# A kernel of two attention layers and four experts: batches pipelined in row tiles, with the causal mask of the maxima added by two 128-row matmuls per pair of heads

## The chip, the cores and the metric

The kernel runs on one core of one Trainium2 chip. The metric is the device time of one execution in microseconds (us), the median of the runs shown. Engines are named TensorE (PE in the profile, with PEld for its weight loads), VectorE (DVE), ScalarE (ACT), GpSimd (POOL) and SyncE (SP, here a queue of transfers).

## The reference

The input x has 8 batches of 512 tokens with 128 channels, in float32. Two layers with residuals follow each other. The first is a retention: layer norm, q, k and v of 16 heads of 8 channels, rotary angles, causal scores with a decay in place of a softmax, a norm per head, and an output projection. The second is a transformer block on the layer norm of the result: RMS norm, causal softmax attention with 16 heads of 8 channels whose q and k are normalised per head, then four experts with a router that keeps two of them. Channels 0 to 31 get neither attention nor expert output.

```python
qk = jnp.einsum('bhtd,bhsd->bhts', q, k) * (1.0 / np.sqrt(DH))
qk = qk * decay[None]
out = jnp.einsum('bhts,bhsd->bhtd', qk, v)
...
scores = jnp.einsum('bhqd,bhkd->bhqk', q, k) * HD ** (-0.5)
scores = jnp.where(causal[None, None], scores, -jnp.inf)
attn = jax.nn.softmax(scores, axis=-1)
...
o2 = _gelu(_gelu(_gelu(xf @ e2_l1.T) @ e2_l2.T) @ e2_l3.T) @ e2_l4.T
moe = wts[:, 0:1] * o0 + wts[:, 1:2] * o1 + wts[:, 2:3] * o2 + wts[:, 3:4] * o3
```

## The kernel before

**Tiles.** The 512 tokens of a batch are NT = 4 tiles of 128. The 16 heads are G = 4 groups of J = 4 heads. A head takes 32 rows of the contraction: q and k are split in a high and a low part, so that the one-pass float type (fp32r) is exact enough, and stand in `stack` as high, low, high, with the negated maximum of the row in a further row (SHIFT = 24). `stacked` transposes this layout with an identity matrix (L441): four matmuls for each group of q and of k, in both layers.

**Scores.** One matmul of 128 rows and 512 columns gives the scores of four heads for one pair of tiles: its moving operand (`qx` or `kx`) is spread in block form by transfers of SyncE, one per head (L1240, L1252), so that the rows of the other heads are zero. In the second layer every causal pair of tiles is computed twice, the queries in the rows for the maxima (L580) and the keys in the rows for the exponents (L593), 10 of each for each group. On the diagonal a second matmul adds the mask: idb times `negb` (L583) or times `negkb` (L596), in bf16, 128 rows and 512 columns. VectorE takes the maxima (L1058), ScalarE the exponents (L789). The maxima of a group are transposed (L602) and go into row SHIFT of `qx` by four small transfers (L1261). `weigh` multiplies the exponents with the values in column tiles of 32 (L560). The first layer does the same with the retained scores (L449), masked by VectorE (L957) and GpSimd (L1159), and `weigh_retained` (L460).

**Order.** All units of the second layer stand in one list, ORDER: the first NU + 14 maxima, then exponents and maxima in turn, then the last exponents. They rotate through four banks of PSUM (`pr`), so TensorE can be up to four units ahead of the engine that reads them. Two banks (`px`) serve what lies beside, one (`ps`) the single steps and one (`po`) the sums of values.

**Batches.** `run` has three stages. `beside_attention(b)` runs the attention of batch b with the down projections of b-1 and the `lead` of b+1 (layer norm, projections, rotation, stack and retained scores of tiles 0 and 1) beside it. `beside_front(b)` runs the rest of the first layer and the normalisations of b up to q and k of the second, with the expert matmuls of b-1 beside it (L629, L644; down projections L666). Batches 1 to 6 run in a hardware loop. Every engine works through its list in order and waits on semaphores, and inverse roots are eleven small VectorE steps (L876 to L881). All inputs of a batch are loaded by ScalarE's queue (L706).

## Time and profile before

| | us |
|---|---|
| median of 3 runs | 1051.71 |
| lowest and highest run | 1051.55, 1053.09 |
| the profiled execution | 1052.72 |
| its span | 1050.9 |
| busy: TensorE, VectorE, ScalarE, GpSimd | 866.0, 682.8, 507.0, 171.4 |
| mean granted TensorE clock, share of full speed | 0.899 |

A row of the profile names an engine, the line of the kernel, the operation, what is written and read, and how often. Times in a timeline are the start from the span's begin and the duration. Ends of matmuls are modelled and durations of neighbouring ones overlap, so what a matmul costs in a stream is read from the distance between starts. A float32 matmul stands there twice, once for each of its two passes, and each pass takes two cycles a column.

### The profile page before, as it was taken

What the parts mean: (1) busy time and instruction counts of PE and PEld (TensorE: products, weight loads), DVE (VectorE), ACT (ScalarE), POOL (GpSimd) and SP (SyncE); (2) the same over time, 40 slices, a digit from 0 to 9 for tenths busy, and PEclk for the clock granted to TensorE, in tenths of its full rate; (3) what the DMA queues carried; (4) which work ended last, traced back from release to release, by engine and by line L of the source; (5) the groups of instructions that cost most, each with busy time, mean ns of one, the idle gap of its engine ahead of it and who ended that gap; (6) DMA issues with size and microseconds to landing.
All of it is one profiled execution on the core that took longest, in us unless ns stands there. A gap on an engine that the chain in (4) does not pass through costs nothing.

```text
span 1050.9 us, 15987 instructions
## 1 busy us (share of the span) xinstructions
PE 866.0 (82%) x4513; PEld 500.2 (48%) x4560; DVE 682.8 (65%) x1825; ACT 507.0 (48%) x1080; POOL 171.4 (16%) x218
## 2 busy tenths in 40 slices
PE   2646897898878897898987897898977989879967
PEld 1524454464435554364543654455543645436434
DVE  6467936788368854789368873688457883578431
ACT  1313473456544474455644465454644556444634
POOL 5310202022010301013020210104020220202002
PEclk9575898899989998899988999799988989889979
DMA  4101210030100301021100301003100201003000
GB/s 142 40 11 24 47 33 20 1 71 13 41 11 0 81 5 46 0 50 31 40 11 0 81 1 40 11 10 71 29 22 0 59 22 40 1 0 81 2 0 11
DMA packets 27893, 31.57 MB, mean 30 GB/s; under 512 B 5184, under 2 KB 16064, under 8 KB 27840
## 3 DMA queue, kind: packets, MB, share of 16 engines
q1 hardware_dynamic: 23616, 28.92, 11.9%
q10 hardware_dynamic: 4224, 2.10, 0.7%
q8 instruction: 14, 0.23, 0.1%
q14 instruction: 39, 0.32, 0.1%
HBM read 5.58 MB, written 2.10 MB: 7 GB/s over the span
## 4 chain that ended last, share of the span: by engine, by line
PE 67%; DVE 20%; issue 6%; ACT 4%; DMA 1%; SPq 0%; DVEq 0%; POOL 0%; ACTq 0%; POOLq 0%
PE ring L593 9%; PE outs L560 8%; PE side L629 8%; DVE mxp L1058 6%; PE side L666 6%; PE ring L580 5%; PE ring L449 4%; PE ring L441 3%; PE side L644 3%; PE outs L460 3%; PE side L441 3%; PE single L435 2%; PE ring L596 2%; PE single L509 2%; PE ring L540 2%
## 5 line engine op out<-in xcount | busy, mean ns | idle before, releaser
L1058 DVE TENSOR_REDUCE mxp<-ring 128x4 f32<-128x512 f32 x320 | 204.8, 684 | 31.6 <-PE ring L580 25.6
L789 ACT ACTIVATE p<-ring 128x512 f32<-128x512 f32 x320 | 173.6, 603 | 67.5 <-PE ring L596 43.6
L593 PE MATMUL ring<-qx,ks 128*128 128x512 f32 x320 | 141.8, 497 | 20.7 <-DVE mxp L1058 19.2
L580 PE MATMUL ring<-kx,qs 128*128 128x512 f32 x320 | 147.3, 509 | 2.5 <-DVE mxp L1058 0.4
L1159 POOL TENSOR_SCALAR_AFFINE_SELECT p<-p 128x512 f32<-128x512 f32 x64 | 39.7, 635 | 311.9 <-ACT p L698 310.8
L593 PEld LDWEIGHTS ring<-qx,ks 128*128 128x128 f32 x320 | 62.4, 201 | 59.2 <-DVE mxp L1058 27.7
L560 PE MATMUL outs<-p,v 128*32 128x512 f32 (+3 forms) x1024 | 87.7, 442 | 0.7
L580 PEld LDWEIGHTS ring<-kx,qs 128*128 128x128 f32 x320 | 63.5, 202 | 37.2 <-DVE mxp L1058 23.8
L1053 DVE COPY oT<-outs 128x512 f32<-128x512 f32 x32 | 22.0, 689 | 89.7 <-PE outs L560 89.7
L435 PE MATMUL single<-sb_t_id,nat 128*128 128x128 f32 x128 | 27.2, 351 | 59.3 <-DVE nat L1086 29.6
L666 PE MATMUL side<-sb_w_dn,h 128*128 128x96 f32 x384 | 51.9, 276 | 6.0 <-ACT h L817 6.0
L1165 POOL TENSOR_TENSOR oT<-oT 128x192 f32<-128x192 f32 x32 | 18.9, 589 | 228.9 <-ACT oT L847 228.3
L435 PEld LDWEIGHTS single<-sb_t_id,nat 128*128 128x128 f32 x128 | 18.0, 176 | 79.7 <-issue 54.9
L666 PEld LDWEIGHTS side<-sb_w_dn,h 128*128 128x128 f32 x384 | 47.8, 192 | 13.8 <-ACT h L817 12.5
L449 PE MATMUL ring<-qx,ks 128*128 128x512 f32 x128 | 49.1, 519 | 3.1 <-DMA qx<-qs 3.1
L957 DVE TENSOR_TENSOR p<-ring,sb_t_tri 128x512 f32<-128x512 f32 x64 | 41.8, 686 | 13.8 <-PE ring L449 13.5
L817 ACT ACTIVATE hB<-side 128x512 f32<-128x512 f32 x32 | 19.1, 597 | 63.2 <-PE side L629 44.3
L698 ACT ACTIVATE p<-ring 128x512 f32<-128x512 f32 x64 | 36.1, 596 | 25.1 <-PE ring L449 24.9
L441 PE MATMUL ring<-idr,stack 128*128 128x128 f32 x256 | 37.4, 295 | 8.3 <-DVE stack L897 7.9
L596 PE MATMUL ring<-negkb,idb 128*128 128x512 bf16 x109 | 44.1, 405 | 0.0
L847 ACT ACTIVATE oT<-side,wts 128x96 f32<-128x96 f32 x128 | 32.3, 351 | 23.0 <-PE side L666 23.0
L560 PEld LDWEIGHTS outs<-p,v 128*32 128x32 f32 x1024 | 22.0, 108 | 43.9 <-issue 24.6
(169 smaller groups left out, 1602.2 us busy)
## 6 DMA issues: line engine op xcount, KB each, us to landing
qx<-qs SPq DMA_DIRECT2D x32, 256.0 KB, 4.6
...
qx<-h SPq DMA_DIRECT2D x128, 2.0 KB
...
```

Of the source, the lines that this page charges most:

```text
L435: last = nc.tensor.transpose(dst[:, t * 128:(t + 1) * 128], src(t), ident[:])
L441: last = nc.tensor.matmul(dst[:, t * 128:(t + 1) * 128], stack[:, s, t, J * g:J * g + J, :].rearrange("p j s -> p (j s)"), idr[:], start=T ...
L449: nc.tensor.matmul(dst[:, :], ks1[:, g, t * 128:(t + 1) * 128], qx[:, g, :, t * 128:(t + 1) * 128], start=True, stop=True)\
L560: last = nc.tensor.matmul(po[32 * j:32 * j + 32, kt * 128:T], v2[:, kt, h:h + SW], p2(kt)[:, j, :], start=kt == 0, stop=kt == NT - 1, skip ...
L580: last = nc.tensor.matmul(dst[:, :], qs[:, g, qt * 128:(qt + 1) * 128], kx[:, g % 2, :, kt * 128:(kt + 1) * 128], start=True, stop=kt < qt)
L593: last = nc.tensor.matmul(dst[:, :], ks[:, g, kt * 128:(kt + 1) * 128], qx[:, g, :, qt * 128:(qt + 1) * 128], start=True, stop=kt < qt)
L596: last = nc.tensor.matmul(dst[:, :], idb[:], negkb[:, :, :], start=False, stop=True)
L629: last = nc.tensor.matmul(dst[:, :], w[:, k * n + m * 128:k * n + (m + 1) * 128], src(k), start=k == 0, stop=k == blocks - 1)
L666: last = nc.tensor.matmul(dst[:, e * CM:(e + 1) * CM], h[:, k, t * 128:(t + 1) * 128], ww[w][:, k * CM:(k + 1) * CM], start=k == 0, stop=k ...
L789: A_(p2(kt)[:, :, (qt - kt) * 128:(qt - kt + 1) * 128], pr[(U_AB + at) % 4][:, :].rearrange("p (j n) -> p j n", j=J), ACT.Exp, scale=float ...
L957: V.tensor_tensor(p1[:, t % 2, g], src[:].rearrange("p (j n) -> p j n", j=J), tri[:].unsqueeze(1).broadcast_to([128, J, 128]), ALU.mult)\
L1058: V.tensor_reduce(mxp[:, qt, :, kt], ring(b, U_AB + at)[:].rearrange("p (j n) -> p j n", j=J), AX.X, ALU.max).then_inc(max_read, 1)
```

## The change

It replaces the three stages by one loop, written out in the program, of 12 iterations (`it` from -2 to 9). Iteration `it` works on five batches at once: `lead` of it+2 (layer norm, projections and rotation of the first layer), the retained scores and `before` of it+1 (rest of the first layer, normalisations), the maxima of `it`, exponents, output and router (`tail`) of it-1, and experts and down projections of it-2. An iteration has NF = 8 places, with experts, retained scores and `retain`, and then 32 steps. In step s TensorE computes one unit of exponents and one of maxima, then what the plan puts there. Exponents of groups 2 and 3 of batch it-1 come in steps 0 to 15, of groups 0 and 1 of batch `it` in steps 16 to 31.

A unit covers two heads and all tiles that a tile of 128 rows needs (128 to 512 columns). Each head has its own row tile of 32 rows (24 or 25 used) and its own bank. So q and k aren't spread in block form; the layout high, low, high comes from 12 transfers for q and 12 for k in each layer (`spread`), of 8 rows each, out of plain transposes whose high part ScalarE and whose low part VectorE or GpSimd writes. The mask of the maxima is two matmuls of 128 rows and 128 columns per unit (idb times `negb`). The exponents' mask is a GpSimd operation on the block of each unit. The maxima have two banks in all (`mb`), as have the exponents (`eb`), and each new unit waits until the last was read; three banks serve the rest. VectorE writes the negated maxima of a row at once. The norm per head takes its mean out with a matmul by `t_centre`. The outputs of two groups are summed in one bank. The diff, cut to its core (in `before` of SyncE, step 19 spreads for layer two; in `lead`, step 26 for layer one):

```diff
-ORDER = MAXIMA[:NU + AHEAD] + mixed(EXPS, MAXIMA[NU + AHEAD:]) + EXPS[(G - 1) * NU - AHEAD:]
...
+NH = J // 2
+CH = C
+GK = NT * NH
+LAG = 2 * GK
+FIRST, LAST = -2, B + 2
+
+WEIGH_AT = {5: (-1, 2, 0), 9: (-1, 2, 1), 13: (-1, 3, 0), 17: (-1, 3, 1), 21: (0, 0, 0), 25: (0, 0, 1), 29: (0, 1, 0)}
+MT_AT = {1: (-1, 3), 9: (0, 0), 17: (0, 1), 25: (0, 2)}
+NF = 8
...
+        mb = pb("maxima", [128, 2, 512])
+        eb = pb("scores", [128, 2, 512])
+        po = pb("outs", [128, 512])
+        px = [pb(f"side{i}", [128, 512]) for i in range(3)]
...
-        pr = [pb(f"ring{i}", [128, 512]) for i in range(4)]
-        ps = pb("single", [128, 512])
-        po = pb("outs", [128, 512])
-        px = [pb(f"side{i}", [128, 512]) for i in range(2)]
...
+            def maxima(b, k):
+                g, qt, hp = k // GK, k % GK // NH, k % NH
+                if k == 0:
+                    pe.wait_ge(spread2_q, count(spread2_q, b, 12 * 16))
+                    pe.wait_ge(spread2_k, count(spread2_k, b, 12 * 16))
+                if count(max_read, b, k) > 0:
+                    pe.wait_ge(max_read, count(max_read, b, k))
+                n = 128 * qt
+                for i in range(2):
+                    rows = slice(SW * (2 * hp + i), SW * (2 * hp + i) + SHIFT)
+                    nc.tensor.matmul(mb[:, i, 0:n + 128], qs[rows, b % 2, g, n:n + 128], ks[rows, b % 2, g, 0:n + 128],
+                                     start=True, stop=False, skip_group_check=True)
+                for i in range(2):
+                    last = nc.tensor.matmul(mb[:, i, n:n + 128], idb[:], negb[:], start=False, stop=True, skip_group_check=True)
+                last.then_inc(m_filled, 1)
...
+            def exponents(it, k):
+                b, g, kt, hp = scores_at(it, k)
+                if not on(b):
+                    return
+                i8 = GK * g + NH * kt + hp
+                if i8 % GK == 0:
+                    pe.wait_ge(shift_ready[g], count(shift_ready[g], b, J * 16))
+                if count(exp_done, b, i8) > 0:
+                    pe.wait_ge(exp_done, count(exp_done, b, i8))
+                n = T - 128 * kt
+                for i in range(2):
+                    rows = slice(SW * (2 * hp + i), SW * (2 * hp + i) + SHIFT + 1)
+                    last = nc.tensor.matmul(eb[:, i, 0:n], ks[rows, b % 2, g, 128 * kt:128 * kt + 128],
+                                            qs[rows, b % 2, g, 128 * kt:T], start=True, stop=True)
+                last.then_inc(e_filled, 1)
...
+            def retained_scores(b, t):
+                if t == 0:
+                    pe.wait_ge(spread1_q, count(spread1_q, b, 12 * 16))
+                    pe.wait_ge(spread1_k, count(spread1_k, b, 12 * 16))
+                at = slice(128 * t, 128 * t + 128)
+                for j in range(J):
+                    dst = side(f"SC{t}{j}", b)
+                    rows = slice(SW * j, SW * j + SHIFT)
+                    for g in range(G):
+                        last = nc.tensor.matmul(dst[:, 128 * g:128 * g + 128], ks1[rows, g, at], qs1[rows, g, at],
+                                                start=True, stop=True)
+                    last.then_inc(side_filled, 1)
...
+                for j in range(J):
+                    for g in range(G):
+                        w = SHIFT + SW * (J * g + j) - D * j
+                        last = nc.tensor.matmul(po[SW * g:SW * g + SW, at], v1x[:, t, w:w + SW],
+                                                p1[:, t % 2, j, 128 * g:128 * g + 128], start=t == 0 and j == 0, stop=j == J - 1,
+                                                skip_group_check=True)
...
+            for it in range(FIRST, LAST):
+                if it == FIRST + 1:
+                    pe.wait_ge(consts_made, 1)
+                    pe.wait_ge(loaded, 16 * (len(ww) + 7 - len(PROJECTION + ROTATION)))
+                for place in range(NF):
+                    if place in (0, 1, 3, 5) and on(it + 1):
+                        if place != 1:
+                            retained_scores(it + 1, (0, 1, 1, 2, 2, 3)[place])
+                    if place == 1:
+                        weigh(it - 1, 1, 1)
+                    if on(it - 2):
+                        experts(it - 2, place)
+                    if place == 1 and on(it + 1):
+                        retained_scores(it + 1, 1)
+                    if place in (2, 4, 6, 7) and on(it + 1):
+                        retain(it + 1, {2: 0, 4: 1, 6: 2, 7: 3}[place])
+                for s in range(G * GK):
+                    exponents(it, s)
+                    if on(it):
+                        maxima(it, s)
+                    if s in WEIGH_AT:
+                        off, g, half = WEIGH_AT[s]
+                        weigh(it + off, g, half)
+                    if s in (0, 2, 4) and on(it - 2):
+                        down(it - 2, s // 2)
+                    if on(it + 1) and s != 17:
+                        before(it + 1, s)
+                    if s == 6 and on(it - 2):
+                        down(it - 2, 3)
+                    if s in MT_AT and on(it + MT_AT[s][0]):
+                        maxima_transposed(it + MT_AT[s][0], MT_AT[s][1])
+                    if on(it + 1) and s == 17:
+                        before(it + 1, s)
+                    if on(it - 1):
+                        tail(it - 1, s)
...
+                g, qt, hp = k // GK, k % GK // NH, k % NH
+                dve.wait_ge(m_filled, count(m_filled, b, k + 1))
+                if k % GK == 0 and b:
+                    dve.wait_ge(mT_ready, count(mT_ready, b - 1, g + 1))
+                V.tensor_reduce(mneg[:, g, 2 * hp:2 * hp + 2, qt], mb[:, :, 0:128 * (qt + 1)], AX.X, ALU.max, negate=True)\
+                    .then_inc(max_read, 1)
...
+            def exponents(it, k):
+                b, g, kt, hp = scores_at(it, k)
+                if not on(b):
+                    return
+                i8 = GK * g + NH * kt + hp
+                pool.wait_ge(exp_done, count(exp_done, b, i8 + 1))
+                diag = p2[kt][:, 2 * hp:2 * hp + 2, 0:128]
+                Q.affine_select(out=diag, in_=diag, compare_op=ALU.is_ge, fill=0.0, base=0, pattern=[[0, 2], [1, 128]],
+                                channel_multiplier=-1).then_inc(exp_masked, 1)
...
+            def spread(dst, parts, order, signal):
 
-                    sp.wait_ge(ring_filled, count(ring_filled, b, U_AB + PLACE["max", g - 2, NU - 1] + 1))
+                    for r, part in enumerate(order):
+                        sp.dma_start(dst[SW * j + D * r:SW * j + D * r + D, :, :].bitcast(f32),
+                                     parts[SW * j:SW * j + SW, part, :]).then_inc(signal, 16)
...
+            def before(b, s):
+                if s == 19:
+                    if b >= 2:
+                        sp.wait_ge(e_filled, count(e_filled, b - 2, G * GK))
+                    sp.wait_ge(low2_ready, count(low2_ready, b, 1))
+                    spread(qs[:, b % 2], qhl, (0, 0, 1), spread2_q)
+                    sp.wait_ge(low2_ready, count(low2_ready, b, 2))
+                    spread(ks[:, b % 2], khl, (0, 1, 0), spread2_k)
+
+            def lead(b, s):
+                if s == 26:
+                    if b:
+                        sp.wait_ge(side_filled, UNIT["SC33", b - 1] + 1)
+                    sp.wait_ge(low1_q, count(low1_q, b, 1))
+                    spread(qs1, qhl, (0, 0, 1), spread1_q)
+                    sp.wait_ge(high1_ready, count(high1_ready, b, 2))
+                    sp.wait_ge(low1_k, count(low1_k, b, 1))
+                    spread(ks1, khl, (0, 1, 0), spread1_k)
```

## Rows read from the trace of the kernel before

**Rows 1.** The page: busy time of the engines; shares of the chain that ended last.
```profile
PE 866.0 (82%) x4513; PEld 500.2 (48%) x4560; DVE 682.8 (65%) x1825; ACT 507.0 (48%) x1080; POOL 171.4 (16%) x218
...
PE 67%; DVE 20%; issue 6%; ACT 4%; DMA 1%; SPq 0%; DVEq 0%; POOL 0%; ACTq 0%; POOLq 0%
```
**Rows 2.** Input loads inside the loop: min/median/max ns, first and last start.
```profile
L706 ACTq MOVE x_in<-x_dram x6: 29/29/29, 170.9 to 779.3; - x6
```
**Rows 3.** Stretches: us, then busy time of the engines, clock, DMA.
```profile
core 0: us, PE busy (x) PEld busy (x) DVE busy (x) ACT busy (x) POOL busy (x), PEclk, DMA share, GB/s
343.40:465.10 121.70, 105.35 (x564) 60.73 (x568) 83.44 (x227) 62.67 (x134) 19.57 (x26) 0.92 0.12 28
416.00:430.00 14.00, 14.00 (x60) 6.56 (x60) 8.13 (x23) 6.19 (x12) 2.72 (x5) 0.79 0.04 12
465.00:523.00 58.00, 53.54 (x333) 29.68 (x338) 38.09 (x66) 35.47 (x79) 12.72 (x16) 1.00 0.23 51
```
**Rows 4.** Timeline (start, us, engine): loads of one stacked transpose.
```profile
460.58 0.53 PEld L441 LDWEIGHTS ring<-idr,stack 128*128 128x128 f32 x4
```
**Rows 5.** Line 1058: min/median/max ns, first and last start; group of line 789.
```profile
L1058 DVE TENSOR_REDUCE mxp<-ring x320: 674/682/695, 102.0 to 985.5; 128x4 f32<-128x512 f32 x160
...
L789 ACT ACTIVATE p<-ring 128x512 f32<-128x512 f32 x320 | 173.6, 603 | 67.5 <-PE ring L596 43.6 <-PE ring L593 13.7 <-remote 5.8
```
**Rows 6.** Timeline: retained scores at two clocks; loads of two matmuls in a stream.
```profile
406.88 1.17 PE L449 MATMUL ring<-qx,ks 128*128 128x512 f32 x4
...
416.16 2.05 PE L449 MATMUL ring<-qx,ks 128*128 128x512 f32 x4
...
512.49 0.42 PEld L593 LDWEIGHTS ring<-qx,ks 128*128 128x128 f32 x2
```
**Rows 7.** Timeline: full array, column tiles of 32, full array again.
```profile
517.86 0.19 PEld L593 LDWEIGHTS ring<-qx,ks 128*128 128x128 f32 x1 [0.21 <-ACT p L789]
518.41 0.19 PEld L560 LDWEIGHTS outs<-p,v 128*32 128x32 f32 x8 [0.37 <-issue]
518.44 1.06 PE L560 MATMUL outs<-p,v 128*32 128x512 f32 x8
...
519.44 0.19 PEld L593 LDWEIGHTS ring<-qx,ks 128*128 128x128 f32 x1 [0.84 <-ACT p L789]
...
520.79 1.56 PE L560 MATMUL outs<-p,v 128*32 128x384 f32 x24
```
**Rows 8.** Timeline: one unit of exponents with its mask, alone.
```profile
484.21 0.50 PE L593 MATMUL ring<-qx,ks 128*128 128x512 f32 x1 [2.76 <-DVE mxp L1058]
...
484.55 0.39 PE L596 MATMUL ring<-negkb,idb 128*128 128x512 bf16 x1
```
**Rows 9.** Timeline: down projections, projections of two tiles, an output projection.
```profile
405.99 1.10 PE L509 MATMUL single<-sb_w_o,chT 128*128 128x96 f32 x8
...
466.53 1.03 PE L666 MATMUL side<-sb_w_dn,h 128*128 128x96 f32 x8
...
475.19 1.45 PE L472 MATMUL side<-sb_w_qkv,chT 128*128 128x384 f32 x4
```
**Rows 10.** Groups by line: steps of inverse roots, busy us, mean ns, idle before.
```profile
L879 DVE TENSOR_TENSOR rs_t<-rs_y 128x4 f32<-128x4 f32 x48 | 7.8, 162 | 1.6
L879 DVE TENSOR_TENSOR rs_t<-rs_y 128x128 f32<-128x128 f32 x24 | 7.0, 293 | 0.8
```
**Rows 11.** Timeline: loads of two successive expert matmul passes of 512 columns.
```profile
443.53 0.19 PEld L629 LDWEIGHTS side<-hA,sb_w_l 128*128 128x128 f32 x1 [0.24 <-issue]
...
443.96 0.19 PEld L629 LDWEIGHTS side<-hA,sb_w_l 128*128 128x128 f32 x1 [0.24 <-issue]
```
**Rows 12.** Line 1252: issues of 64 KB transfers, min/median/max ns, and their landing.
```profile
L1252 SPq DMA_DIRECT2D kx<-ks x96: 507/590/1634, 96.6 to 969.4; - x96
...
DMA to landing us min/median/max: 2.0/2.0/3.4
```
**Rows 13.** Timeline: a small VectorE step beside a clearing by GpSimd.
```profile
5.09 6.93 POOL L1226 MEMSET qx<- 128x8192 f32 x1
...
5.77 6.28 DVE L906 TENSOR_SCALAR rs_v<-mv_in 128x4 f32<-128x4 f32 x1
```

1730 lines of the change are left out of this document (769 added, 961 removed).

## The prediction

> **What bounds the kernel now.** I read the page first. TensorE is busy 82% of the span and holds 67% of the chain that ended last, VectorE 20% [rows 1]. The input loads give the period: the six loads inside the loop lie 170.9 to 779.3 us, so one batch takes (779.3 - 170.9)/5 = 121.7 us, and 8 x 121.7 = 974 leaves 77 us for the filling and emptying of the pipeline [rows 2]. The table of stretches shows where TensorE isn't pressed: in one period it is busy 105.4 of 121.7 us. Before attention, where normalisations and experts run (416 to 430 for one), its clock is 0.79; within attention (465 to 523) it is busy 53.5 of 58 us at clock 1.00 [rows 3]. So the kernel is TensorE-bound in attention and bound by chains across engines before it.
>
> **What is removed.** The stacked transposes (68 per batch at 0.53/4 = 0.13 us) cost 9 us of TensorE per batch [rows 4]. Also gone are their copies on VectorE and ScalarE, the second step of the maxima and six blocks of transposes. The maxima (40 units a batch at 684 ns = 27.4 us) and the exponents (40 x 603 ns = 24.1 us) become 32 larger units each, over the same 20480 elements per partition [rows 5]. From 684 ns for 512 elements I take 0.15 us fixed plus 1.04 ns an element, so 256, 512, 768 and 1024 elements cost 0.42, 0.69, 0.95 and 1.22 us, 26 us a batch. ScalarE likewise needs 23 us. So neither reader gains much.
>
> **What a step of the new kernel costs.** Attention is 32 steps per iteration. A step has one pair of row-tile matmuls for the exponents, one pair for the maxima, then the two 128-row masks. The maxima have one pair of PSUM banks, so each unit waits until VectorE has read the last; the exponents wait likewise for ScalarE. Before, four banks turned. No row of before shows a row tile, so I bound it. A load and a 128-column matmul take 0.13 us together [rows 4], and two full matmuls of 512 columns in a row 0.42, so 512 columns stream in 0.21 us [rows 6]. A pair of mean length 320 costs two loads, 0.26, and 0.13 of streaming if both run side by side: two pairs 0.78, less one hidden load 0.65. Column tiles do run side by side: eight matmuls of 512 columns take 1.06 us [rows 7]. The masks are 2 x 0.05 plus a load of 0.05.
> The masks need the whole array and the scores a quarter of its rows, so the array changes shape twice a step. The nearest rows are the changes to and from column tiles: the last load before the change ends at 518.05, the first column-tile load starts at 518.41, and the next full load at 519.44, when the eight matmuls have ended (518.44 + 1.06 = 519.50); it isn't hidden [rows 7]. I price going in at 0.14 and coming out at 0.24, of which 0.1 is a load already counted: 0.29 a step. Sum: 0.65 + 0.16 + 0.29 = 1.1 us. Ends: 0.8 without any cost of the change of shape, 1.4 if the pairs also run one after another (+0.27).
> A sentence of the Trainium skill speaks against this change: "Mode switching requires drain" (TensorEngine Tiling (Array Packing), Key Properties). By that rule the step is 1.1 us, without it 0.8; the trace's column tiles agree, with load to load 0.36 us going in.
> On VectorE's path a unit is: release, loads and maxima pair 0.5, masks with change and pipeline 0.38, then the reduction 0.82: 1.75 us on average. The row of before for the same path is a maxima or exponent matmul from 484.21 to the masks' end at 484.94, 0.73 us [rows 8]. Before, four banks hid this; now only other work can.
>
> **TensorE beside the steps.** Down projections: 64 matmuls at 0.125 (eight in 1.03) = 8.0 us [rows 9]. Weighing: 1.06 us for the first tile of a group and 1.56 for the other three [rows 7], 10.5 a batch, of which 7 of 8 halves lie in the steps: 10 with changes of shape. Projections 4 x 1.45 = 5.8, eleven blocks of transposes, taken like the stacked ones at 0.53: 5.8, wo2 1.1, wo1 and the new centring matmul likewise [rows 9], gate 1.2, states 0.8, four transposed maxima 1.4. Sum 36; with 32 x 1.1 = 35, TensorE has 71 us in the steps.
> VectorE beside the reductions has 34 us, mostly chains of small steps: eleven of 0.17 to 0.29 us plus 0.035 between them per inverse root, five of those [rows 10]. So 60 us, and ScalarE 44.
>
> **Why the steps take longer than 71.** Each engine works through its own list in order, and TensorE can be only one step ahead of VectorE. So I walk the steps and take the longer engine of each stretch. Steps 0 to 6: TensorE, 7 x 1.1 = 7.7 and beside them 12.9 (down projections 8.0, centring and wo1 2.1, half a weighing 1.9, a transpose and a maxima transpose 0.9), plus 1 waiting for ScalarE between ON and WO1: 21.5. Steps 7 to 16: VectorE, reductions 8.2 and 17.8 of normalisation (sum and moments 2.0, root 2.6, two scalings 2.2, moments 1.3, root 2.4, scaling 1.1, sums 1.7, root 3.3, product 1.2; passes over 512 elements at 0.69), plus two units that nothing covers, 0.94 each: 28. Steps 17 to 31: TensorE, 16.5 and beside them 16.4 (weighings 5.5, transposes 4.9, projections 2.9, wo2 1.1, gate 1.2, states 0.8), plus 4 where steps 18 and 25 belong to VectorE: 37. Together 86.5 us.
>
> **The places before the steps.** Experts: 38 matmul passes at 0.43 = 16.3 us [rows 11]. Retained scores: 64 loads and 128-column matmuls in row tiles, 0.13 each: 8.5 (before 16 at 0.19 = 3). Retained values 4 x 1.4 with changes of shape, the last weighing 1.3: 32, with buffer waits 33.
> But the first thing TensorE does there is to wait for the spread of q and k: 24 transfers, which SyncE issues in step 26, where before there were 4 or 8 at a time. One issue takes 590 ns, landing 2.0 us [rows 12]. 24 x 0.59 + 2.0 = 16.2 us after step 26's ScalarE and GpSimd work (at about 76.5): 92.7, while the steps end at 86.5. TensorE stands for 6 us, and everything behind the wait with it. In before, the four score matmuls that came after a stretch with TensorE pauses took 2.05 instead of 1.17 us [rows 6], its lower clock level: 2 us more. An iteration is 86.5 + 6 + 35 = 127.5 us against 121.7.
>
> **The ends.** There are 12 iterations, -2 to 9. The first maxima begin after two iterations that are chains, estimated by the same rows: the spread lands at 50, retained scores 16, normalisations and projections 38 at low clock, spread 2 and then spread 1 of the next batch (29 us of issues): 147 us, against 102.0 before [rows 5]. Iteration 0: 75. Iteration 1, no experts: 102. Iterations 2 to 5: 4 x 127.5 = 510. Iteration 6, no spread for a later batch: 120. Iteration 7, no normalisations beside: 22 + 64 = 86. Iterations 8 and 9, experts and down projections twice with little beside: 94. Sum 1134 us of span. The profiled run of before took 1052.72 with a span of 1050.9, the median is 1051.71: I add 1 and say 1135.
>
> **Rivals.**
> Faster (R1): the engines overlap more than my walk allows. What the normalisations cost in chains before (the stretch at clock 0.79 [rows 3]) really lies beside attention work now, and steps take TensorE's 71 us instead of 86.5, with a few for waits: 73. Seven iterations have full steps: 1135 - 7 x 13.5 = 1040; if the change of shape costs half too, 256 x 0.145 less: 1003. I say 1010. It decides in the steps: 1135 - 1051.7 = 83 us over 8 x 32 steps, so from 0.33 us a step less than I say, the new kernel is faster. For it: VectorE's total falls from 84 to 72 us a batch, and TensorE's is no higher. Against it: one buffer each, where four stood.
> Slower still (R2): the two matmuls of a pair don't run side by side, 256 x 0.27 = 69 more: 1200. Only column tiles speak against it.
> R3: the waits and chains are as I say but the transfers stall nothing, since the previous work hides them: 7 x 8 less, 1080. It needs issues of under 0.3 us; none of 96 was under 507 ns [rows 12].
> R4: the change of shape is free, the rest as I say: 256 x 0.29 less, 1060. I count its share with R3.
> That the change doesn't do what it says is excluded by the diff: two full-row mask matmuls per pair stand there.
> One more unknown has both signs: GpSimd masks every exponent block now, 32 a batch, and small VectorE steps were held up while GpSimd ran (one step took 6.28 us beside a clearing of 6.93) [rows 13]. I take 0, the ends are -1 and +6 us an iteration. And the loop is written out: issue holds 6% of the chain, 63 us [rows 1], which bounds from above what the jumps of the hardware loop can cost; I take 0 here too, and against the other end that the longer program is fetched late at places.
>
> **Chances.** Forecast (1085 to 1180) 0.52; R1 0.25; R2 0.09; R3 and R4 0.11; within 0.2% of before 0.03. A measurement of this kernel can tell about 0.2% from no change. Faster 0.25, same 0.03, slower 0.72. The range runs from 1005, which takes in most of R1, to 1195.
>
> **What would show it.** Right: a period of 127 us between output sums; TensorE idle of 4 to 8 us before the first retained scores, ended by the spread's transfers; reductions waiting for the mask matmuls; loads of the masks' weights starting only 0.1 us after the row tiles' end; first maxima near 147. Wrong: loads hidden under the other shape's matmuls; VectorE or ScalarE busy in nearly every step; matmuls of a pair that start one full length apart (R2); a period under 117 (R1).

## The result, and the profile after

The changed kernel takes 1330.68 us (median of four runs, 1328.57 to 1346.79) against 1051.68 us for the kernel before in the same job: a ratio of 1.268, 95% interval 1.258 to 1.278. It is slower, as forecast, but by 279 us where I had said 83, and 1330 lies far outside my range of 1005 to 1195. One run of one experiment below (the second of bank) fell in a slower state, at a lower granted clock, and is left out of its comparison. All of this section is read from one profiled execution of 1330.73 us with a span of 1328.6.

The page of the changed kernel, by the lines that answer to [rows 1]: busy time, the clock in 40 slices, the queue of the transfers (packets, MB, share of 16 engines), and the chain that ended last by engine and by line.

```profile
PE 927.6 (70%) x5904; PEld 562.4 (42%) x5904; DVE 581.6 (44%) x1433; ACT 444.0 (33%) x912; POOL 276.3 (21%) x483
...
q1 hardware_dynamic: 29152, 33.19, 15.9%
...
PE 47%; DVE 18%; SPq 13%; issue 9%; DMA 8%; ACT 4%; POOL 1%; POOLq 0%; ACTq 0%; DVEq 0%
SPq L1126 12%; PE side L443 12%; PE outs L384 5%; DVE mneg L810 5%; DMA ks<-h 4%; PE side L404 4%; PE scores L365 4%; PE side L479 4%; PE outs L422 3%; PE maxima L347 3%; PE side L334 3%; DMA qs<-h 3%; PE maxima L350 2%; PE side L434 2%; PE side L429 2%
```

No engine that held the chain has grown much: VectorE fell from 683 to 582 us busy, TensorE rose from 866 to 928. GpSimd rose from 171 to 276, with 1% of the chain. But in the chain stands what had 1% before: SyncE's issues of the spread (line 1126, 12%) and its landings (`ks<-h` and `qs<-h`, 7%). That is a fifth of the time, some 250 us of chain, on the way of transfers.

The output stores, the first and the fifth (start, us, engine and line), give the period: (1069.61 - 476.59)/4 = 148.3 us, where the forecast was 127.5 and before had 121.7 [rows 2].

```profile
476.59 0.39 SPq L1157 DMA_DIRECT2D out_dram<-yout  x1
...
1069.61 0.38 SPq L1157 DMA_DIRECT2D out_dram<-yout  x1
```

The first maxima start at 188.2 us. I had said 147; before it was 102.0 [rows 5].

```profile
L810 DVE TENSOR_REDUCE mneg<-maxima x256: 417/820/1229, 188.2 to 1232.0; 128x2 f32<-128x256 f32 x32, 128x2 f32<-128x512 f32 x32, 128x2 f32<-128x768 f32 x32, 128x2 f32<-128x1024 f32 x32
```

Stretches of one iteration, as [rows 3]: the places with experts and retained scores, the 32 steps, the wait behind them, and the last part of that wait one iteration earlier.

```profile
core 0: us, PE busy (x) PEld busy (x) DVE busy (x) ACT busy (x) POOL busy (x), PEclk, DMA share, GB/s
706.40:744.20 37.80, 35.66 (x254) 19.32 (x254) 10.00 (x26) 14.89 (x23) 5.08 (x8) 0.81 0.00 1
744.20:840.00 95.80, 75.09 (x480) 47.35 (x476) 60.62 (x150) 39.16 (x88) 27.35 (x48) 0.74 0.17 26
840.00:855.40 15.40, 1.95 (x12) 0.93 (x12) 2.45 (x2) 0.87 (x3) 0.81 (x2) 0.61 0.61 77
...
697.60:706.40 8.80, 0.00 (x0) 0.00 (x0) 0.00 (x0) 0.00 (x0) 0.00 (x0) 0.50 0.65 79
```

38 us of places, 96 of steps, 15 of nothing. In the last row no engine does anything: the transfers alone run, at 79 GB/s. These are the spread's and the 256 KB of the next input, which SyncE issues right behind it. The spread alone shows in the middle of the second layer's (812 to 826 us), at 68 GB/s:

```profile
812.00:826.00 14.00, 10.42 (x61) 7.07 (x61) 8.57 (x23) 3.57 (x12) 4.81 (x6) 0.63 0.53 68
```

The clock shown in the wait is 0.50, its lower level of 1.2 GHz; it was 0.92 over a period before.

The queue of SyncE over the second half of an iteration shows both spreads, 12 transfers of q and 12 of k each:

```profile
802.50 8.49 SPq L1126 DMA_DIRECT2D qs<-h  x12
811.04 8.43 SPq L1126 DMA_DIRECT2D ks<-h  x12
...
831.72 8.49 SPq L1126 DMA_DIRECT2D qs<-h  x12
840.32 8.43 SPq L1126 DMA_DIRECT2D ks<-h  x12
```

and these are the two that wait for them, ScalarE in step 25, then TensorE in front of the retained scores (the brackets: idle before it, and what ended it):

```profile
827.59 0.60 ACT L712 ACTIVATE qT<-side 128x512 f32<-128x512 f32 x1 [6.07 <-DMA ks<-h]
```

```profile
706.44 1.14 PE L404 MATMUL side<-qs,ks 24*128 24x128 f32 x12 [16.31 <-issue]
...
856.51 1.14 PE L404 MATMUL side<-qs,ks 24*128 24x128 f32 x12 [13.50 <-issue]
```

The last issue of the second layer's spread ends at 819.47, and ScalarE goes on at 827.59: a landing 8.1 us behind the last issue. For the first layer's it is 848.75 and 856.51, 7.8 us. The 64 KB transfers of before landed in 2.0 [rows 12]. ScalarE waits at all since both layers put their high and low halves into the same buffers (`qhl, khl = h0, h3`), so layer 1 may not write until layer 2's spread has left. The wait at the retained scores is put down to issue, but the queue shows what it is: in all eight batches it ends 7.8 to 8.9 us after the last issue.

Summed over the run, TensorE's waits are these (us, times, longest):

```profile
PE maxima L347 <- DVE mneg L810: 107.7, 84, 2.6
PE side L404 <- issue: 87.6, 6, 16.3
PE side L404 <- DMA ks<-h: 66.0, 2, 39.6
```

154 us stand in front of the retained scores. ScalarE has 47.4 us more in step 25.

### The profile page after: what moved, and what is told of

Its sections match the earlier page's. It is cut to its first block, busy times and chain, and to the rows that moved or that the text cites. A ratio compares the mean times of both kernels' runs of the same rounds, so it can differ in the third digit from the quotient of the medians.

```text
span 1328.6 us, 16021 instructions
## 1 busy us (share of the span) xinstructions
PE 927.6 (70%) x5904; PEld 562.4 (42%) x5904; DVE 581.6 (44%) x1433; ACT 444.0 (33%) x912; POOL 276.3 (21%) x483
## 2 busy tenths in 40 slices
DMA packets 29228, 34.19 MB, mean 26 GB/s; under 512 B 5344, under 2 KB 16352, under 8 KB 29152
## 3 DMA queue, kind: packets, MB, share of 16 engines
q1 hardware_dynamic: 29152, 33.19, 15.9%
## 4 chain that ended last, share of the span: by engine, by line
PE 47%; DVE 18%; SPq 13%; issue 9%; DMA 8%; ACT 4%; POOL 1%; POOLq 0%; ACTq 0%; DVEq 0%
SPq L1126 12%; PE side L443 12%; PE outs L384 5%; DVE mneg L810 5%; DMA ks<-h 4%; PE side L404 4%; PE scores L365 4%; PE side L479 4%; PE outs L422 3%; PE maxima L347 3%; PE side L334 3%; DMA qs<-h 3%; PE maxima L350 2%; PE side L434 2%; PE side L429 2%
## 5 line engine op out<-in xcount | busy, mean ns | idle before, releaser
L810 DVE TENSOR_REDUCE mneg<-maxima 128x2 f32<-128x256 f32 (+3 forms) x256 | 211.1, 825 | 318.7 <-PE maxima L350 316.9
L616 ACT ACTIVATE p<-scores 128x1024 f32<-128x1024 f32 (+3 forms) x256 | 180.4, 705 | 247.3 <-PE scores L365 246.6
L1037 POOL TENSOR_SCALAR_AFFINE_SELECT p<-p 128x256 f32<-128x256 f32 x256 | 107.3, 419 | 580.2 <-ACT p L616 580.2
L347 PE MATMUL maxima<-ks,qs 24*128 24x384 f32 (+3 forms) x512 | 116.0, 450 | 108.1 <-DVE mneg L810 107.7
L404 PE MATMUL side<-qs,ks 24*128 24x128 f32 x512 | 62.1, 358 | 171.9 <-issue 87.6
L365 PE MATMUL scores<-qs,ks 25*128 25x256 f32 (+3 forms) x512 | 130.6, 507 | 50.1 <-ACT p L616 49.5
L384 PE MATMUL outs<-p,v2x 128*32 128x512 f32 (+3 forms) x1024 | 124.3, 626 | 1.0 <-POOL p L1037 1.0
L347 PEld LDWEIGHTS maxima<-ks,qs 24*128 24x128 f32 x512 | 63.2, 244 | 140.5 <-DVE mneg L810 137.9
L365 PEld LDWEIGHTS scores<-qs,ks 25*128 25x128 f32 x512 | 58.5, 225 | 115.9 <-ACT p L616 63.9
L350 PE MATMUL maxima<-negb,idb 128*128 128x128 bf16 x512 | 86.4, 261 | 0.0
```

The lines of the kernel that those rows point to most:

```text
L347: nc.tensor.matmul(mb[:, i, 0:n + 128], qs[rows, b % 2, g, n:n + 128], ks[rows, b % 2, g, 0:n + 128], start=True, stop=False, skip_group_c ...
L350: last = nc.tensor.matmul(mb[:, i, n:n + 128], idb[:], negb[:], start=False, stop=True, skip_group_check=True)
L365: last = nc.tensor.matmul(eb[:, i, 0:n], ks[rows, b % 2, g, 128 * kt:128 * kt + 128], qs[rows, b % 2, g, 128 * kt:T], start=True, stop=True)
L384: last = nc.tensor.matmul(po[SW * j:SW * j + SW, 128 * kt:T], v2x[:, b % 3, kt, at:at + SW], p2[kt][:, j, :], start=a == 0 and kt == 0, st ...
L404: last = nc.tensor.matmul(dst[:, 128 * g:128 * g + 128], ks1[rows, g, at], qs1[rows, g, at], start=True, stop=True)
L616: A_(p2[kt][:, 2 * hp:2 * hp + 2, :], eb[:, :, 0:n], ACT.Exp, scale=float(D) ** -0.5).then_inc(exp_done, 1)
```

## Experiments on the transfers

My theory after this reading: the excess over my forecast is the spread, through its slow landing and its shared staging, and what these waits do to the clock behind them. The rivals: the steps themselves cost more than I said, and the wait only shows it; or the issuing queue, not the transfers, is the limit.

**A third of the transfers (third).** For each head group only the first of the three parts goes out.

```diff
-                    for r, part in enumerate(order):
+                    for r, part in list(enumerate(order))[:1]:
```

> Each spread moves a third: 4 transfers of q and 4 of k in place of 12 and 12, so two thirds of the rows of q and k are left at zero and the output isn't the reference's. Two clearings at the start are added. My theory (the transfers are the excess: 24 issues of 0.67 us and a landing 8 us after the last, which stop TensorE for 16 us in front of the retained scores and ScalarE for 6 us in step 25): 8 issues of 0.67 are 5.4 us, landing about 3, both waits shrink under 2 us, the period falls from 149 to 127-130 us and the time to about 1150 (1120 to 1180), near my forecast of 1135. Rival (the steps themselves, with one pair of banks each and a low clock of their own, hold the time; another late input takes the place of each wait): not under 1230.

Measured: 1187.43 us (ratio 1.128, 1.116 to 1.141), period 126.6 us. The wait is gone but for 1.5 us:

```profile
600.00 1.14 PE L404 MATMUL side<-qs,ks 24*128 24x128 f32 x12 [1.46 <-issue]
```

143 us of the 279 thus hang on two thirds of the spread. The rest of the theory's number, 1150, was too low by 37.

**The same bytes to 32 partitions (wide).**

```diff
-                        sp.dma_start(dst[SW * j + D * r:SW * j + D * r + D, :, :].bitcast(f32),
+                        sp.dma_start(dst[SW * j:SW * j + SW, r, :].bitcast(f32),
```

> The same count of transfers and the same bytes, 64 KB each, but each goes from 32 partitions to 32 partitions and not to 8, as the transfers of the kernel before did. Rows land in the wrong places and the exponent's scale is a hundredth, so the output isn't the reference's; two clearings at the start are added. Theory A (four packets of one transfer into the same partition are what makes them slow; before, the rate was 151 GB/s, now 79): rate back near 150 GB/s, landing 2 to 3 us after the last issue, issues under 0.6 us, waits of 16 and 6 us become about 8 and 1, time about 1240. Theory B (the rate depends on the number and size of the packets, not on where they go): 79 GB/s and 1330 as now.

Measured: 1255.26 us (1.193, 1.189 to 1.196), period 136.5, wait in front of the scores 7.05. Theory A's numbers hold, though not its reason (stride, below, still puts four packets into each target partition and is fast): with the same megabytes the queue's packets took far less engine time, 10.3% of a span of 1254 us in place of 15.9% of 1329.

```profile
q1 hardware_dynamic: 32224, 33.20, 10.3%
```

**Staging of its own (own).** Layer 1 uses two tiles that are idle then and one new one; layer 2 keeps h0 and h3.

```diff
-        qhl, khl = h0, h3
+        qhl2, khl2 = (h0[:, 0], h0[:, 1]), (h3[:, 0], h3[:, 1])
...
+        qhl1, khl1 = (xnT, chT), (khl[:, 0], khl[:, 1])
```

> The high and low halves of q and k of the first layer get a place of their own in SBUF (two tiles that are idle then and one new one); nothing waits any longer for the second layer's spread before it writes them. My theory: ScalarE's wait of 6.1 us in step 25 and the wait at the third place go; the spread of the first layer is issued 6 us earlier and lands 6 us earlier, if the queue has drained by then; 7 x 6 = 43 us less: 1288 (1275 to 1300). Rival (the queue is still full of the second layer's transfers, so what ScalarE no longer waits for TensorE waits for in front of the retained scores): 1320 to 1335.

Measured: 1307.80 us (1.243, 1.232 to 1.254), period 141.9, so 6.4 us less per iteration as said. ScalarE's wait for the transfer in step 25 is gone from the list, and that in front of the scores is as long as before, since everything in front of it moved with it:

```profile
694.57 1.14 PE L406 MATMUL side<-qs,ks 24*128 24x128 f32 x12 [16.11 <-issue]
```

The total fell by 23 and not by 43; one of its two runs was at 1303, the other at 1312.

**Work in the wait (fill).** Ten matmuls of 512 columns on constants in front of the wait.

> In front of the wait for the spread TensorE gets ten matmuls of 512 columns on constants whose result nobody reads: two passes of 0.43 us each warm, so 8.6 us warm and up to 17 us at the lower clock, in a wait of 16.3 us. Theory (the pause itself lowers the granted clock of the places behind it, where it is 0.79 and the first loads take 0.85 in place of 0.43 us): the places fall from 38 to about 34 us, 1300 (1290 to 1315). Rival (the clock is low for another reason, as the small row-tile matmuls of the steps): no gain, 1325 to 1345.

Measured: 1324.42 us (1.258, 1.255 to 1.262), period 143.3. The matmuls fill the wait (2.9 and 3.3 us are left of it where I looked), and the first twelve score matmuls behind it then took 0.68 us in one iteration and 1.14 in another. In all it gave 6 us and not 30, but not evenly. The period is 5 us shorter, about what the theory said. The places of iterations 2 to 6 took 33 to 34 us each (clock 0.90 to 0.95), where the changed kernel had 34 in two of them and 38 (clock 0.81) in three. From the first maxima of the last batch to the end it took 189 us in place of 172, at a clock of 0.66 in place of 0.76, and this took most of the gain back. Is it the pause that makes the places slow? Against it stand two other runs of this document: own had 34 to 35 us in four of these five iterations, each behind a wait of 15 or 16 us, and six had 38 in one of them with no wait at all. From score to score own and six take 142.9 and 127.0 us, a difference of 15.8 for waits of 15 to 16. So in the full iterations a pause costs about its own length; that it also slows the places isn't shown.

**Experts in front of the scores (first).** The staging of own, and the retained scores moved from place 0 to place 4, behind the experts' up projections.

```diff
-NF = 8
+NF = 10
+RS = {4: 0, 5: 1, 7: 2, 8: 3}
+RT = {6: 0, 7: 1, 8: 2, 9: 3}
```

> The first layer's own place for its halves (as in own) and all of the experts' up projections up to the fourth place in front of the retained scores, instead of behind or between them: TensorE has about 12 to 16 us of work while the transfers run. My theory (the 16 us in front of the retained scores are a wait for the transfers and nothing else): period 143 down to 128-130 us, the wait under 3 us, 1307 - 8 x 13 = about 1205 (1185 to 1230). Rival (scores, their copies and masks and the retained values then form a chain that nothing covers): half of the gain at most, 1255 or more.

Measured: 1249.26 us (1.187, 1.182 to 1.191), period 132.5. 58 us came back against own; my 1205 was too good. The waits in front of the scores from the third batch on fell from 93 us to 19 over six iterations, 74 less, and TensorE's idle time as a whole fell by 75 (377 to 302). So no new idle time took their place, as the rival's uncovered chain would have. What was lost again is busy time: the same 5904 matmuls took 943 us in place of 924.

**k's transfers on a second queue (twoq).** ScalarE issues k's twelve while SyncE issues q's.

```diff
+                    if s == 26 and on(it + 2):
...
+                        spread_on(act, ks1, khl, (0, 1, 0), spread1_k)
```

> q's transfers stay on SyncE's queue, k's are issued by ScalarE on its own: 12 issues each side by side, same bytes and same shapes. Theory A (a limit of all transfers of this shape together, 79 GB/s: 1.57 MB need 20 us however they are issued): the landing comes 20 us after the start in place of 25, the wait in front of the scores about 11, but ScalarE stands for 2 x 12 x 0.6 us in each iteration: 1300 (1280 to 1330). Theory B (one queue's limit): rate doubles, wait about 5 us, 1230 to 1260.

Measured: 1353.28 us (1.285, 1.278 to 1.293), slower than the changed kernel. In one iteration both queues issued side by side, from 701.5 to 710.7, and TensorE went on at 728.75: 27 us after the start, where one queue alone took from 831.7 to 856.5, 25 us. So neither the issues nor the queue bound it: 1.57 MB of transfers of this form take 25 us. And ScalarE stood for its issues. The Trainium skill says so in advance: issuing from several engines saves only the sequencers' time, since all transfers run on the same 16 DMA engines (DMA: Bandwidth & Descriptors, Issuing engines are not separate DMA queues); this run agrees.

**Rows placed otherwise (six, twelve, stride).** The three parts of a row tile needn't lie one behind the other. With row 4d + r for dimension d of part r, and row 31 for the shift, a whole part goes out in one transfer, since the source's 128 partitions come in the order that the target needs. These three compute the whole result.

```diff
-                for j in range(J):
-                    for r, part in enumerate(order):
-                        sp.dma_start(dst[SW * j + D * r:SW * j + D * r + D, :, :].bitcast(f32),
-                                     parts[SW * j:SW * j + SW, part, :]).then_inc(signal, 16)
+                for r, part in enumerate(order):
+                    sp.dma_start(dst[r:128:4, :, :].bitcast(f32), parts[:, part, :]).then_inc(signal, 64)
```

> The whole computation, with another layout of the row tiles: row 4d + r holds dimension d of part r, and row 31 the shift, so that one transfer takes a part of q or k from all 128 partitions to every fourth partition (32 of them): 3 transfers of 256 KB in place of 12 of 64 KB, 6 in place of 24 per spread. The contraction runs over 31 rows of a tile in place of 24. Theory A (few target partitions per transfer and the count of issues are what costs): 1.57 MB in about 12 us, wait in front of the scores 3 to 5 us, none in step 25: about 1200 (1180 to 1225). Theory B (four packets in a row into one partition are slow, wherever the transfer goes else): 79 GB/s, 20 us, wait 11 us: about 1280.

Measured: 1168.58 us (1.113, 1.109 to 1.117), period 127.0, below every value that I had given. The six transfers are issued in 3.9 us, and by 578 the transfers are over:

```profile
571.45 1.90 SPq L1128 DMA_DIRECT2D qs<-h  x3
573.44 1.88 SPq L1128 DMA_DIRECT2D ks<-h  x3
```

```profile
core 0: us, PE busy (x) PEld busy (x) DVE busy (x) ACT busy (x) POOL busy (x), PEclk, DMA share, GB/s
571.40:578.00 6.60, 5.37 (x38) 2.49 (x38) 3.81 (x10) 1.61 (x3) 1.23 (x3) 0.81 0.79 278
...
581.00:615.00 34.00, 31.32 (x238) 17.27 (x240) 11.12 (x27) 14.89 (x23) 5.08 (x8) 0.90 0.00 1
615.00:707.00 92.00, 74.81 (x512) 46.88 (x500) 60.69 (x151) 40.00 (x91) 28.17 (x50) 0.78 0.12 41
```

278 GB/s in place of 79, both with the next input's load among them. Nothing waits for a transfer in the period any more: 34 us of places and 92 of steps are all.

In twelve each transfer takes one g as well, 64 KB from 32 partitions to 32:

> The same layout as in six, but one transfer for each part and each g: 12 of 64 KB for q and 12 for k as in the changed kernel, each from 32 partitions to 32 partitions, one packet into each. It is the kernel wide with the rows where they belong. Theory A: 24 issues of 0.63 us and a landing under 2 us after the last, wait 7 us, 1250 to 1260 as wide. Rival (steps of 4 between partitions cost something too): over 1280.

Measured: 1242.54 us (1.183, 1.178 to 1.188), wait 6.93 us: bound by its 24 issues, as forecast.

In both, the number of target partitions and their distance changed together. stride keeps the changed kernel's transfers, 24 of 64 KB from 32 partitions to 8, and moves only the 8 apart:

```diff
-                        sp.dma_start(dst[SW * j + D * r:SW * j + D * r + D, :, :].bitcast(f32),
+                        sp.dma_start(dst[SW * j + r:SW * j + SW:4, :, :].bitcast(f32),
```

> The changed kernel's 12 and 12 transfers of 64 KB, each from the same 32 partitions to 8, but to every fourth partition of a row tile and not to 8 neighbours (the layout of six, with its 31 rows). Theory P (neighbouring partitions share a way into SBUF, so what counts is how far the 8 lie apart): only the issues bound it, 24 x 0.63 to 0.67 us, landing under 3 us after the last, wait in front of the scores about 7, time as twelve and wide: 1240 to 1255. Theory N (the number of target partitions per transfer, or the four packets into each, counts): 79 GB/s as now, landing 8 us after the last issue, 1325 to 1345.

Measured: 1243.71 us (1.182, 1.177 to 1.188). The queue's share halves, and the scores start 1.5 us after the last issue (637.22 + 8.43 = 645.65):

```profile
q1 hardware_dynamic: 29152, 33.19, 7.4%
```

```profile
637.22 8.43 SPq L1129 DMA_DIRECT2D ks<-h  x12
```

```profile
647.16 1.14 PE L404 MATMUL side<-qs,ks 31*128 31x128 f32 x12 [8.80 <-issue]
```

This settles it for the landing. Number, size, source and count of target partitions are as they were; what made the landing slow was that the eight target partitions are neighbours. By the queue's share and its 29152 packets in both, a packet took 0.12 us on average with neighbours and 0.05 without (an estimate from the two pages of the profile). The Trainium skill has the rule that I should have looked up: the rate depends on how many of SBUF's 16 ports the partitions reach, and partitions that differ only in their two lowest bits or by 32 share one (SBUF — State Buffer, Door 1: The DMA port swizzle). By it eight neighbours reach two ports, and every fourth partition of 32 reaches eight. By its 27.2 GB/s a port two ports would give 54 GB/s as an estimate; the trace has 68 for the spread alone, with transfers to other neighbours under way together.

**Both together (best).** six with first:

> Six and first together: six transfers of 256 KB per spread, the first layer's halves in a place of their own, experts in front of the retained scores. By my theory nothing is left to wait for in front of the scores, but the chain of scores, masks and retained values is less covered (in first it kept the period at 133 us with a wait of 3): 125 to 130 us a period, 1180 (1160 to 1205). Against the kernel before, 1052: still some 12% slower, since steps and places alone take 126 us and the start and end are longer.

Measured: 1180.11 us (1.124, 1.116 to 1.132), period 130.5. It is 12 us slower than six alone, with intervals that touch, and its period is 3.5 us longer. With nothing left to wait for, moving the scores gains nothing. As in first it isn't idle time that grew: TensorE's fell from 252 to 245 us, while the same matmuls took 937 us in place of 915, at a mean clock of 0.727 in place of 0.745.

## Experiments on the steps

What is left is why a period without a wait takes 126 us, and which of my prices for a step was right.

**The mask in eight row-tile matmuls (mask8), and none at all (nomask).** These two start from the changed kernel, not from six.

```diff
-                for i in range(2):
-                    last = nc.tensor.matmul(mb[:, i, n:n + 128], idb[:], negb[:], start=False, stop=True, skip_group_check=True)
+                for r in range(J):
+                    for i in range(2):
+                        part = slice(SW * (2 * hp + i), SW * (2 * hp + i) + SW)
+                        last = nc.tensor.matmul(mb[:, i, n:n + 128], idb[part, r, :], negb[part, r, :], start=False,
+                                                stop=r == J - 1, skip_group_check=True)
```

> The mask of the maxima as eight row-tile matmuls per pair (32 rows each, four per head, in that head's own row tile, two heads side by side) in place of two of 128 rows; the constants are laid out for it. The array then never changes its shape within a step. If the change of shape costs the 0.29 us a step that I priced it at, less the six more matmuls (three more pairs at 0.05 to 0.13): between 256 x 0.14 less (1295) and 256 x 0.1 more (1356). If a change of shape is nearly free, as the trace of the changed kernel looks (0.57 us from the exponents' first matmul to the next load after the masks): 256 x 0.15 to 0.3 us more in the steps that TensorE holds: 1350 to 1390.

> No mask of the maxima at all: the two 128-row matmuls are left out, so the maxima also range over the keys that the mask forbids, and the shape of the array changes only for other work. It bounds all that the masks and their change of shape can cost. By my prediction (0.16 + 0.29 = 0.45 us a step): 256 x 0.45 = 115 us less, 1215, if TensorE held every step; as only some 18 of 32 steps are TensorE's, at least 1265. If the change is nearly free and the two matmuls cost 0.1 to 0.15 us: 1295 to 1320.

Measured: mask8 1359.80 us (1.292, 1.285 to 1.299), nomask 1314.75 (1.249, 1.239 to 1.259). So the two full-row masks with their changes of shape cost about 16 us in all, 0.06 us a step (the intervals of the two kernels just touch), and are worth some 29 us against eight row tiles. My 0.45 us a step is refuted as a part of the time. Without the masks TensorE was busy 42 us less (886 for 928), but idle 30 us more, and its clock was 0.688 in place of 0.707: most of what it saved it then waited. Weight loads of step 0, then the first of the down projections (engine PEld, the bracket is idle time before):

```profile
744.16 0.18 PEld L365 LDWEIGHTS scores<-qs,ks 25*128 25x128 f32 x2 [0.20 <-issue]
744.27 0.19 PEld L347 LDWEIGHTS maxima<-ks,qs 24*128 24x128 f32 x2
744.65 0.11 PEld L350 LDWEIGHTS maxima<-negb,idb 128*128 128x128 bf16 x2 [0.20 <-issue]
744.73 0.97 PEld L479 LDWEIGHTS side<-sb_w_dn,h 128*128 128x128 f32 x8
```

From the first load of the step to the next work's first load are 0.57 us: exponents, maxima, both masks and one change of shape. The mask's load waits 0.20 us; the load behind it comes after 0.08, since that is the full array's shape again. I had priced two changes a step, and 1.1 us. The way back shows where the next step's row tiles follow the masks at once (here with 512 columns of maxima):

```profile
938.34 0.18 PEld L347 LDWEIGHTS maxima<-ks,qs 24*128 24x128 f32 x2 [0.93 <-DVE mneg L810]
938.77 0.11 PEld L350 LDWEIGHTS maxima<-negb,idb 128*128 128x128 bf16 x2 [0.24 <-issue]
938.98 0.18 PEld L365 LDWEIGHTS scores<-qs,ks 25*128 25x128 f32 x2
```

There the next load comes 0.21 us after the masks' first, 0.13 later than in step 0. So both changes exist, 0.2 and 0.13 us at the full clock. And all of this is at the full clock: at its lower level (0.50) a step of 256 and 384 columns took 0.92 us, from 1080.30 to 1081.22.

**Half the columns of each reduction (six_half).** From here on the base is six. The shifts are then maxima over half the keys.

```diff
-                V.tensor_reduce(mneg[:, g, 2 * hp:2 * hp + 2, qt], mb[:, :, 0:128 * (qt + 1)], AX.X, ALU.max, negate=True)\
+                V.tensor_reduce(mneg[:, g, 2 * hp:2 * hp + 2, qt], mb[:, :, 0:64 * (qt + 1)], AX.X, ALU.max, negate=True)\
```

> The kernel six (1169 us), but each reduction of the maxima reads only the first half of its columns, so the shifts are those of half the keys. A reduction takes 0.49 us in place of 0.82 on average. My walk (VectorE holds steps 7 to 16 and two more, 12 of 32, TensorE the rest): 8 x 12 x 0.33 = 32 us less, 1137 (1125 to 1145). Rival 1 (with one pair of banks the reduction is on the path of every step): 256 x 0.33 = 84 less, 1085. Rival 2 (TensorE holds nearly all): not under 1160.

Measured: 1092.51 us (1.040, 1.036 to 1.044). The reductions take 125.7 us in place of 210.9 (group of the line: busy, mean ns, idle before):

```profile
L810 DVE TENSOR_REDUCE mneg<-maxima 128x2 f32<-128x128 f32 (+3 forms) x256 | 125.7, 491 | 317.1 <-PE maxima L350 315.1
```

85 us less of reductions, 76 us less of time: close to rival 1 in number and far from my walk's 32. But the trace doesn't bear out rival 1's reason, a reduction on the path of every step. TensorE's waits for a reduction in front of the maxima (us, times, longest), in six and then in six_half:

```profile
PE maxima L347 <- DVE mneg L810: 114.4, 84, 2.6
```

```profile
PE maxima L347 <- DVE mneg L810: 81.9, 81, 2.8
```

TensorE waits in 84 of 256 steps, and these waits fell by 32 us, my walk's number. All idle time of TensorE fell by 28 us (251.6 to 224.0). The other 48 us are busy time (914.9 to 867.2) of the same 5904 matmuls: the mean granted clock rose from 0.745 to 0.784, and 914.9 x 0.745 / 0.784 is 869. The shorter reductions are all that was changed, so both parts come from them; that the clock rose because TensorE paused less is my reading.

**Six more full matmuls a step (six_heavy).**

```diff
+                    for _ in range(3):
+                        nc.tensor.matmul(mb[:, i, n:n + 128], zerob[:], negb[:], start=False, stop=False, skip_group_check=True)
```

> The kernel six with six more 128-row matmuls of 128 columns in each step, which add zeros to the maxima (0.3 us a step of TensorE, 256 x 0.33 = 84 us if all of it were on the path). My walk (TensorE holds 20 of 32 steps, and each reduction starts later by them in the others too): 50 to 84 us more, 1220 to 1250. Rival (the array's low clock, 0.78 in the steps, comes from its small row-tile matmuls; with more full ones the clock rises and gives part back): under 1200, and the granted clock in the steps above 0.85.

Measured: 1198.01 us (1.140, 1.136 to 1.145), 29 us more, with 54 us more of TensorE busy. The steps of one iteration:

```profile
633.00:724.00 91.00, 79.64 (x646) 56.45 (x649) 57.55 (x147) 39.29 (x88) 26.99 (x48) 0.82 0.11 41
```

The granted clock in them is 0.82 where six had 0.78; not the 0.85 that the rival wanted, but it points its way, and the time is under 1200 as it said. Of the 54 us more of busy time 25 didn't show, since TensorE's idle time fell by as much (251.6 to 226.4): they lay in waits. What the clock gave back is inside the 54; an exponents' matmul, for one, took 468 ns in place of 495. Whether the full shape or only the added work raised the clock isn't separated.

**No exponent masks on GpSimd (third_nopool).** Base third.

> The kernel third (a third of the transfers, 1187 us) without GpSimd's 256 masks of the exponents, so these blocks stay unmasked. What I took as 0 with ends of -1 and +6 us an iteration: if VectorE's small steps are held up by GpSimd's masks (a step of 0.69 us takes 1.05 on average now): 8 x 4 = 32 us less, 1155 (1140 to 1165). Rival (they lie beside waits anyway): 1180 to 1190.

Measured: 1159.54 us (1.104, 1.099 to 1.110), 28 us less. But the period is as it was, 127.2 against 126.6 us; the gain lies ahead of the first store (399.2 against 404.6) and behind the fifth. Most of the latter, 15 us, lies behind the first maxima of the last batch, where the clock was 0.79 in place of 0.71. Small VectorE steps were indeed held up (the line of third, then that of third_nopool):

```profile
L793 DVE TENSOR_TENSOR rt_tail<-ry_tail 128x4 f32<-128x4 f32 x24 | 11.4, 476 | 0.8
```

```profile
L792 DVE TENSOR_TENSOR rt_tail<-ry_tail 128x4 f32<-128x4 f32 x24 | 3.9, 162 | 0.8
```

but the period of the full iterations didn't gain by it.

**Handing over the maxima by bank (bank, bank_big).** One head's matmul and mask, a signal, then the other head's; two reductions. In bank for all steps, in bank_big for those of 384 and 512 columns.

```diff
-                for i in range(2):
-                    last = nc.tensor.matmul(mb[:, i, n:n + 128], idb[:], negb[:], start=False, stop=True, skip_group_check=True)
-                last.then_inc(m_filled, 1)
+                    nc.tensor.matmul(mb[:, i, n:n + 128], idb[:], negb[:], start=False, stop=True, skip_group_check=True)\
+                        .then_inc(m_filled, 1)
```

> The kernel six (1169 us) with the maxima handed over by bank: one head's matmul and mask, a signal, then the other head's; two reductions of one head each, 512 in place of 256, and TensorE waits for one bank only. Theory A (the whole pair's turn is the chain: fill 0.5, masks 0.38, reduction 0.82 one after another): filling one bank lies beside reading the other, 0.2 to 0.4 us a step less, less 0.15 us for the second reduction's fixed part: 1130 (1110 to 1150). Theory B (VectorE's own work holds the steps): 256 x 0.15 = 38 us more, 1205. Between: nothing changes, 1169.

> The same, but by bank only where a head has 384 or 512 columns (half of the steps), where a reduction is 0.95 or 1.22 us; the small ones go as a pair. Theory A: most of the gain with half of the added fixed part: 1125 (1105 to 1145). Theory B: 128 x 0.15 = 19 us more, 1188.

Measured: bank 1230.37 us in its profiled run and 1282.84 in the other, bank_big 1213.10 (1.154, 1.150 to 1.157): 62 (by one run) and 45 us more than six, worse than both theories' ends. The experiment changed more than I meant. Weight loads of a step in bank:

```profile
702.48 0.18 PEld L353 LDWEIGHTS maxima<-ks,qs 31*128 31x128 f32 x1
702.91 0.10 PEld L356 LDWEIGHTS maxima<-negb,idb 128*128 128x128 bf16 x1 [0.24 <-issue]
703.08 0.18 PEld L353 LDWEIGHTS maxima<-ks,qs 31*128 31x128 f32 x1
```

The mask between the heads keeps them from running side by side: with 512 columns 0.60 us per head from load to load (702.48 to 703.08), 1.2 for the two, where the changed kernel has 0.64 for the maxima's pair of 512 columns and both masks (938.34 to 938.98). TensorE is busy 1056 us in place of 915. So it says nothing on the turn by bank. It measures three things together: the two heads one after another, one more change of shape each way a step, and 256 more reductions.

## Why the prediction was wrong

The spans of the forecast, of the changed kernel, of stride and of six, by the start of the first maxima and then by the first retained score of each iteration (behind the wait, so the parts are cut a little later than in my sum):

| part | forecast | changed | stride | six |
|---|---|---|---|---|
| up to the first maxima | 147 | 188.2 | 172.5 | 139.1 |
| iteration 0 | 75 | 101.6 | 89.6 | 80.5 |
| iteration 1 | 102 | 128.4 | 119.0 | 109.4 |
| iterations 2 to 5 | 4 x 127.5 | 4 x 147.2 | 4 x 133.9 | 4 x 127.0 |
| iterations 6 to 9 | 300 | 321.7 | 327.3 | 329.4 |
| span | 1134 | 1328.6 | 1243.8 | 1166.5 |

**The step that failed is the landing.** "One issue takes 590 ns, landing 2.0 us" gave 24 x 0.59 + 2.0 = 16.2 us. It took 24 x 0.71 + 8 = 25. I used the row of transfers to 32 partitions for transfers to 8 neighbours, as if 64 KB were 64 KB. [rows 12] has the size, not the form. No bound was kept: I held both ends of TensorE's step and none of the landing, the one term that turned out four times its price. With nothing but the landing mended (stride, 1.5 us) the time is 1244: the landing and what hangs on it are 87 of the 196 us by which I was off.

**The other 109 us are steps and ends.** In stride 26 us of them lie in iterations 2 to 5 (steps of 91 us for my 86.5, a wait of 8.8 for my 6), 25 before the first maxima, 32 in iterations 0 and 1, and 27 in the last four. In iterations 0 and 1 the clock was 0.51 in the places and 0.64 and 0.75 in the steps, where my rows were mostly taken at full speed; how much of the 109 this is, no run separates.

**A wait that I did not see.** The second layer's spread is issued in step 19 and holds h0 and h3, which the first layer's halves need in step 25. With my landing it would have been gone by then; with the true one ScalarE stands for 6 us, and the second spread starts that much later. Waits of 16 and 6 us an iteration, against my 6, and two longer ones in the filling of the pipeline (26.4 and 39.6), are nearly all that changed has over six: 162 us for the same computation. 87 of these go with the landing (stride), the other 75 with the count of issues. I had the two long waits in my start as well, with my price; the start was 41 us too short, and 16 of them go with the landing.

**The price of a step was too high, and its clock was missing.** 1.1 us foretold. At the full clock a step of 512 and 128 columns took 0.57 where full-array work follows, and some 0.13 more where row tiles follow; at the lower level 0.92 where full-array work follows. Too high were the loads: I put 0.13 us for each of four, while the two loads of a pair take 0.18 together and the next pair's follow after 0.11. So the two heads do run side by side, and R2 falls. The change of shape, 0.29 a step by my price, is about 0.2 going in and 0.13 coming back in TensorE's own stream. The rule of the Trainium skill that a change of mode drains the array (TensorEngine Tiling (Array Packing), Key Properties) agrees with that 0.20. But little of it reaches the time: nomask saves 0.06 a step where I had 0.45 for masks and change. R4, "the change of shape is free", comes near this in the time, though not in the stream; its gain of 74 us was not there to be had.

**The walk came out near its sum by two errors.** Steps of 86.5 us against some 91 in six. The price of a step was too high, and the clock that I took as full was 0.78. The first made TensorE's part too long, the second too short: 71 us foretold, 75 measured. How the walk shares the steps between TensorE and VectorE is not refuted: six_half's waits fell by the 32 us that it gave. What it lacks is that the clock rose as the waits fell, which gave 48 us more.

**What held.** The places: 34 to 38 us in both the changed kernel and six, 34 at a clock of 0.90 and 38 at 0.81; 35 foretold. The reductions' 0.42, 0.69, 0.95 and 1.22 us, measured 0.42 to 1.23. GpSimd's masks at 0 for the full iterations. The TensorE idle in front of the retained scores, ended by the transfers, though 14 to 16 us and not 4 to 8. R3, no stall at all, I put at 1080; six, where nothing stalls, measured 1169. Of these 89 us 4 x 7.5 = 30 lie in iterations 2 to 5 (127.0 against 119.5), and 29 or more in the last four.

**The rivals.** R1 rested on VectorE's total falling, and VectorE's total fell; totals say little where transfers stall both engines and where each waits for the other in part of the steps. My chance of 0.25 for faster had no place in the profile.

The best version with the whole computation, six, is still 11% slower than the kernel before. Its period is 5 us longer, 8 x 5.3 = 42 us, and filling and emptying the pipeline takes 1166.5 - 8 x 127.0 = 150 us against 77. A deeper pipeline over eight batches pays for its twelve iterations.
